# Softmax denominators: the last two key blocks summed on ScalarE out of the maximum pass

## Chip, core and metric

One core of a Trainium2 chip. The metric is the device time of one execution in microseconds (us), as the median of several executions; the profile is of one more execution of the same program.

## What is computed

The input is x, two images of 256 channels and 64x64 pixels. Layer 0 is attention over the 4096 pixels with 8 heads of 32 channels, followed by a masked mix with x; layer 1 is a chain of convolutions. What matters here:

```python
q = proj(Wq, bq) / math.sqrt(hd)          # (16, 4096, 32): 2 images x 8 heads
k = proj(Wk, bk)
v = proj(Wv, bv)
attn = jax.nn.softmax(jnp.einsum('bnd,bmd->bnm', q, k), axis=-1)
fuse = jnp.einsum('bnm,bmd->bnd', attn, v)
```

All of it is float32. The softmax of a query n needs the largest score over all 4096 keys m, and the sum of the exponentials over all keys.

## The kernel before

The program has a setup and projection phase, the attention phase (from about 230 to 3660 us) and an image phase with the convolutions. The change touches only the attention phase.

**Units.** Two heads are worked on together (a pair), for 512 queries at a time. That makes 8 pairs x 8 chunks = 64 units, and every unit has the same work:

- The maximum pass ("m" in the order): for each of 2 heads and 4 groups of 128 queries (8 sub-blocks, called hn) one matmul for each of 8 blocks of 512 keys, so 64 matmuls of 128 queries x 512 keys into PSUM (L654-659). They rotate through four banks, `mx`. VectorE reduces each to a column of maxima (L831), and when all 64 are there one small reduction makes the negated maxima (L836). SyncE then moves them with eight DMAs of 128 single numbers each into an extra row of the queries (`row`, L549-557), so that the score matmuls come out with the maximum subtracted.
- The scores ("s"): 64 matmuls of 128 keys x 512 queries (L645-651), which rotate through three banks, `st`. ScalarE turns each into probabilities in SBUF with an Exp (L786); the probabilities lie in a ring of 16 key tiles x 2 heads.
- The values ("V", L661-671): 16 steps, each the four matmuls of two key tiles and two heads, written as 32 columns each and accumulated in the one bank `acc`. Every such matmul stands in the trace as two instructions, so a V has eight.
- The sums ("S", L673-691): the denominators. GpSimd adds the probability tiles up in groups `GROUPS = [4,4,4,4,4,4,2,2]` (20 adds of 128x1024, L505), which covers 28 of the 32 key tiles; the four tiles left over are taken as they are. A matmul by ones then sums over the keys: 6 steps of the size of a V, into the same bank `acc`.

After the last V ScalarE copies the numerators out of `acc` (L761, two copies, after score `NUM_AFTER`), after the last S the denominators (L766, after score `DEN_AFTER`). The denominators go through DRAM (L563, L565), VectorE adds their parts and takes the reciprocal (L812, L815, placed in its own stream at block `INVERT`), and GpSimd scales the numerators (L859, L862, after add `SCALE_AFTER`).

**Order.** TensorE's program is written out by hand in the string `ORDER` (L388), one letter for each step, the same for every unit. It runs ahead: at its start `SCORES_AHEAD` scores of this unit and `BLOCKS_AHEAD` maximum blocks of the next unit have been done already, so its later letters belong to the next unit's scores and to the maximum blocks of the unit after that. Each engine works strictly through its own stream; semaphores are waited for in it.

```python
def max_block(v, p, gp, j):
    pe.wait_ge(mx_taken, MAXMM * v + j + 1)      # bank j % 4 has been reduced
...
act.wait_ge(scores, TILES * u + i + 1)           # score i is in its bank
if h == 0:
    buffer_free(u, s)                            # the ring slot has been used
```

SyncE's stream for a unit (L580-595) is: store and reload the previous unit's denominators (`normalize`), then the eight DMAs of `row`, the loads of later queries, the store of a finished unit.

## Time and profile before

| | us |
|---|---|
| median of 3 runs (4120.0 to 4120.87) | 4120.01 |
| the profiled execution | 4121.6 |
| its span, first to last instruction | 4119.8 |

| engine | busy, us | share of the span |
|---|---|---|
| TensorE matmul (PE) | 3956.2 | 96% |
| TensorE weight load (PEld) | 2046.8 | 50% |
| VectorE (DVE) | 2992.0 | 73% |
| ScalarE (ACT) | 2377.2 | 58% |
| GpSimd (POOL) | 3263.9 | 79% |

How to read it: L831 is line 831 of the kernel; busy times leave out waits; matmuls are pipelined, so that a matmul's row lasts longer than the distance to the next one, and the distance between two starts is what it costs. A row of the timeline may merge several instructions of one kind (x12), as one stretch from the start of the first. The clock is the one granted to TensorE: 1.00 is 2.4 GHz, 0.50 is 1.2 GHz.

### The profile page before, as it was taken

The page shows a single profiled execution, that of the slowest core. Times are in us where ns is not written, and L with a number is a line of the kernel's source. Part 1 is how long each engine was busy: PE and PEld are TensorE (multiplying, and loading weights), DVE is VectorE, ACT ScalarE, POOL GpSimd, SP SyncE. Part 2 cuts the span into 40 slices and gives each one's busy share as a digit, 9 for nine tenths or more (in the row PEclk, how much of TensorE's full clock was granted, in tenths as well). Part 3 has the DMA queues.
Part 4 walks back from the last instruction along what each step waited for, and adds up shares of the span by engine and source line. Part 5 has one row for each costly group of instructions (what it writes and reads, how often), then busy time and mean ns, then how long its engine had stood idle before and what let it go on. Part 6 is the DMA issues. An engine that isn't in the chain of part 4 may idle for free. (4 is left out here: it accounts for less than half of the span.)

```text
span 4119.8 us, 82469 instructions
## 1 busy us (share of the span) xinstructions
PE 3956.2 (96%) x20853; PEld 2046.8 (50%) x20853; DVE 2992.0 (73%) x5094; ACT 2377.2 (58%) x4488; POOL 3263.9 (79%) x1488
## 2 busy tenths in 40 slices
PE   7979999999999999999999999999999999959797
PEld 4535555555555555555555555555555555424343
DVE  3257777777777777777777777777777777518989
ACT  1216666666666666666666666666666666621213
POOL 3428999999999999999999999999999999940000
PEclk9959999999999999999999999999999999979898
DMA  6941110111011101110111011101110000022021
GB/s 199 283 116 40 39 24 22 30 39 31 22 33 42 31 19 32 42 32 22 31 42 32 22 33 42 31 22 32 42 32 22 22 22 21 10 58 76 26 77 41
DMA packets 223398, 188.86 MB, mean 46 GB/s; under 512 B 124434, under 2 KB 149188, under 8 KB 222916
## 3 DMA queue, kind: packets, MB, share of 16 engines
q1 hardware_dynamic: 223108, 185.67, 16.9%
q8 instruction: 100, 1.64, 0.2%
q14 instruction: 190, 1.56, 0.1%
HBM read 124.06 MB, written 61.21 MB: 45 GB/s over the span
## 5 line engine op out<-in xcount | busy, mean ns | idle before, releaser
L831 DVE TENSOR_REDUCE block_max<-mx 128x1 f32<-128x512 f32 x4096 | 2513.7, 681 | 798.6 <-PE mx L657 788.9
L786 ACT ACTIVATE prob<-st 128x512 f32<-128x512 f32 x4096 | 2140.4, 607 | 1152.9 <-PE st L650 1141.0
L505 POOL TENSOR_TENSOR prob_sum<-prob_sum,prob 128x1024 f32<-128x1024 f32 x768 | 1819.6, 2386 | 10.3 <-PE acc L689 10.2
L650 PE MATMUL st<-queries,keys 97*128 97x512 f32 x4096 | 1589.9, 410 | 5.4 <-issue 2.9
L657 PE MATMUL mx<-keys,max_queries 96*128 96x512 f32 x4096 | 1557.5, 412 | 27.3 <-DMA keys<-k_scratch 27.2
L505 POOL TENSOR_TENSOR prob_sum<-prob 128x1024 f32<-128x1024 f32 x512 | 1220.2, 2383 | 224.4 <-PE acc L689 162.9
L650 PEld LDWEIGHTS st<-queries,keys 97*128 97x128 f32 x4096 | 768.5, 189 | 611.4 <-ACT prob L786 352.7
L669 PE MATMUL acc<-prob,values 128*32 128x512 f32 x8192 | 1000.2, 600 | 0.0
L657 PEld LDWEIGHTS mx<-keys,max_queries 96*128 96x128 f32 x4096 | 781.8, 192 | 374.1 <-issue 134.0
L669 PEld LDWEIGHTS acc<-prob,values 128*32 128x32 f32 x8192 | 207.5, 109 | 449.5 <-issue 260.4
L689 PE MATMUL acc<-prob_sum,ones 128*32 128x512 f32 x2048 | 234.8, 599 | 5.3 <-ACT num_part L761 4.7
L366 POOL TENSOR_TENSOR low<-full,high 128x512 fp32r<-128x512 f32 x64 | 81.3, 1270 | 130.0 <-DVE high L347 130.0
L1260 DVE SCALAR_TENSOR_TENSOR conv<-o,dtaps,conv 128x512 f32<-128x512 f32 x256 | 170.4, 738 | 6.4 <-ACT conv L1145 6.4
L1035 PE MATMUL front<-xf,wfT 128*128 128x512 f32 x256 | 115.7, 607 | 40.5 <-DVE wfT L1308 36.6
L1127 ACT ACTIVATE edge<-conv,nshift,nscale 128x512 f32 (+1 forms) x32 | 24.3, 806 | 193.4 <-DVE conv L1226 193.4
L689 PEld LDWEIGHTS acc<-prob_sum,ones 128*32 128x32 f32 x2048 | 60.2, 110 | 145.8 <-issue 137.1
L335 ACT ACTIVATE full<-pq,bqs 128x512 f32<-128x512 f32 x64 | 44.0, 687 | 150.1 <-PE pq L310 150.1
L689 PE MATMUL acc<-prob,ones 128*32 128x512 f32 x1024 | 121.6, 592 | 0.0
L1073 PE MATMUL back<-conv,baT 128*128 128x512 f32 x128 | 68.1, 681 | 45.5 <-DVE conv L1260 45.5
L1226 DVE SCALAR_TENSOR_TENSOR conv<-y,etaps,conv 128x512 f32<-128x512 f32 x160 | 107.3, 745 | 0.0
L347 DVE CAST high<-full 128x512 fp32r<-128x512 f32 x64 | 27.3, 427 | 109.1 <-ACT full L335 109.1
L1035 PEld LDWEIGHTS front<-xf,wfT 128*128 128x128 f32 x256 | 49.7, 195 | 104.9 <-issue 102.8
(106 smaller groups left out, 1193.8 us busy)
## 6 DMA issues: line engine op xcount, KB each, us to landing
max_queries<-q_scratch SPq DMA_DIRECT2D x384, 64.0 KB, 1.9
queries<-q_scratch SPq DMA_DIRECT2D x384, 64.0 KB, 1.9
keys<-k_scratch SPq DMA_DIRECT2D x168, 128.0 KB, 2.5
x<-in_x SPq DMA_DIRECT2D x18, 512.0 KB, 4.3
q_scratch<-high SPq DMA_DIRECT2D x32, 256.0 KB, 4.3
k_scratch<-high SPq DMA_DIRECT2D x16, 512.0 KB, 4.9
q_scratch<-low SPq DMA_DIRECT2D x32, 256.0 KB, 5.1
k_scratch<-low SPq DMA_DIRECT2D x16, 512.0 KB, 4.9
```

What stands on the lines that cost most here:

```text
L366: nc.gpsimd.tensor_tensor(low[p][:, k, :], full[p][:, k, :], high[p][:, k, :].bitcast(F32), ALU.subtract).then_inc(low_ready, 1)
L505: nc.gpsimd.tensor_tensor(psum[k][:, :, :], a, prob[:, (first + i) % RING, :, :], ALU.add).then_inc(added[False], 1)
L650: nc.tensor.matmul(st[bank(i, p)][:, :], kk[gp][:, h, s * P:(s + 1) * P], qq[p][:, h, :], start=True, stop=True).then_inc(scores, 1)
L657: nc.tensor.matmul(mx[j % MAX_BANKS][:, :], qm[p][:, h, ns * P:(ns + 1) * P], kk[gp][0:SPLIT, h, blk * CH:(blk + 1) * CH], start=True, sto ...
L669: mm = nc.tensor.matmul(acc[HD * i:HD * (i + 1), :], vv[gp][:, h, 2 * q + a, :], prob[:, (2 * q + a) % RING, h, :], start=(q == 0), stop=( ...
L689: mm = nc.tensor.matmul(acc[HD * n:HD * (n + 1), :], ones[:, :], src[a][:, h, :], start=(i == 0), stop=(i == SUMS - 1))
L786: nc.scalar.activation(prob[:, s % RING, h, :], st[bank(i, p)][:, :], ACT.Exp).then_inc(exp_done, 1)
L831: nc.vector.tensor_reduce(bmax[p][:, j // MB, j % MB:j % MB + 1], mx[j % MAX_BANKS][:, :], AX.X, ALU.max).then_inc(mx_taken, 1)
L1035: mm = nc.tensor.matmul(front[p][ot][:, :], keep["wf"][:, kt, ot * P:(ot + 1) * P], xf[p][:, kt, :], start=(kt == 0), stop=(kt == 2 * CT - 1))
L1073: mm = nc.tensor.matmul(back[p][ot][:, :], keep["ba"][:, kt, ot * P:(ot + 1) * P], conv[p][:, kt, :], start=(kt == 0), stop=(kt == CT - 1))
L1226: nc.vector.scalar_tensor_tensor(out=as_rows(conv[p][:, ct, :]), in0=inner(y, ct, c, k=k), scalar=keep["etaps"][:, ct, k:k + 1], in1=as_ro ...
L1260: nc.vector.scalar_tensor_tensor(out=dst, in0=inner(o1, ct, c, k=i + 1), scalar=keep["dtaps"][:, ct, i + 1:i + 2], in1=dst, op0=ALU.mult, ...
```

## The change

ScalarE sums the last two key blocks (blocks 6 and 7 of each hn, 1024 keys) straight from the maximum pass. For this the four `mx` banks become one tensor. VectorE reduces blocks 0 to 5 one by one, and 6 and 7 in one instruction of 1024 columns, all of them negated; right after it, still within the same hn, it reduces the seven columns to that hn's negated maximum. ScalarE then takes one Exp over the two banks (1024 columns) with that maximum as bias, writes it back into the same two banks and gives the sum out as an accumulated column (`sum_tail`). TensorE may overwrite these two banks only when that Exp has finished. The eight columns of a unit go to DRAM with one DMA of 128x8 single numbers, and are added as a third part of the denominator. In return the key tiles 24 to 31 fall out of the sums: GpSimd has 6 groups and 18 adds, and TensorE 3 S steps. The values still use all 32 tiles. The negated maxima are buffered twice. The order is written anew.

```diff
-GROUPS = [4, 4, 4, 4, 4, 4, 2, 2]
+GROUPS = [4, 4, 4, 4, 4, 4]
-PLAIN = MT - sum(GROUPS)
+TAIL = 2
+SUMMED = MT - TAIL * NSUB
+PLAIN = SUMMED - sum(GROUPS)
+HN = 2 * NSUB
+TAKES = MB - TAIL + 1
-ORDER = ("ssmmmsmsVsmsmsmmsmsmsVsmssmmsmsmmssmVsmsmsmsmsmsmsmsVVsmsmsmsmsmsmsmsmsVVms"
-         "mssmmmsmsmVsmsmsmsmmsmssVVVmssmsmmsmsmsmsVVVVmsmsmsmsmsmmssmsmVmmsmssSSSSSS")
-SCORES_AHEAD = 18
+ORDER = ("msmVVVmssmsmmsmsmsmsmsVVsmsmsmsmsmsmsmsmsVVsmsmsmsmsmsmsmsmsVVmsmsmsmsmsm"
+         "smsmsVVVsmmssmmsmsmsVsssmmVmsmsmsmsmmssmVVsmsmsmssmmmssmmSSSmsmsmssmmsmsms")
+SCORES_AHEAD = 23
-INVERT = 61
-NUM_AFTER, DEN_AFTER = 14, 18
-SCALE_AFTER = 17
+INVERT = 57
+NUM_AFTER, DEN_AFTER = 12, 15
+SCALE_AFTER = 12
+TAIL_AHEAD = 0
+TAIL_AFTER = [0, 8, 15, 23, 30, 39, 48, 57]
+TAIL_FIRST = BLOCKS_AHEAD // MB
...
-        dcol = sb("den_col", [P, 2, 2 * CH // P])
+        dcol = sb("den_col", [P, 3, 2 * CH // P])
-        mx = [ctx.enter_context(nc.psum_tensor(f"mx{i}", [P, CH], F32)) for i in range(MAX_BANKS)]
+        mx = ctx.enter_context(nc.psum_tensor("mx", [P, MAX_BANKS, CH], F32))
...
             def row(u, p):
-                sp.wait_ge(nmax_ready, u + 1)
+                sp.wait_ge(nmax_ready, HN * (u + 1))
...
+                tail = scratch["den"][bass.ds(u, 1), 4 * CH:6 * CH]
+                sp.wait_ge(tail_summed, HN * (u + 1))
+                sp.dma_start(tail.rearrange("a (i n) -> n (a i)", n=P), part[p][:, :],
+                             allow_slow_non_contiguous=True).then_inc(part_stored, 16)
...
             def normalize(v):
...
                 sp.wait_ge(den_stored, 16 * (v + 2))
-                sp.dma_start(dcol[:, :, :], row.rearrange("a (e p k) -> (a p) e k", e=2, p=P)).then_inc(dcol_loaded, 16)
+                sp.wait_ge(part_stored, 16 * (v + 2))
+                sp.dma_start(dcol[:, :, :], row.rearrange("a (e p k) -> (a p) e k", e=3, p=P)).then_inc(dcol_loaded, 16)
...
-            def max_block(v, p, gp, j):
-                pe.wait_ge(mx_taken, MAXMM * v + j + 1)
+            def max_block(v, p, gp, j, first=False):
+                last, older = (j - MAX_BANKS) // MB, (j - MAX_BANKS) % MB
+                if older < MB - TAIL:
+                    pe.wait_ge(mx_taken, TAKES * HN * v + (TAKES * (last + 1) + older + 1))
+                elif j >= MB or not first:
+                    pe.wait_ge(tail_summed, HN * v + (last + 1))
...
-                            pe.wait_ge(row_loaded, ROW_INC * (u + 3))
+                            pe.wait_ge(row_loaded, ROW_INC * (u + 2))
...
+            def sum_tail(v, p, hn, first=False):
+                if hn == 0 and not first:
+                    act.wait_ge(part_stored, 16 * v)
+                if hn or not first:
+                    act.wait_ge(tail_summed, HN * v + hn)
+                act.wait_ge(nmax_ready, HN * v + hn + 1)
+                nc.scalar.activation(mx[:, MAX_BANKS - TAIL:MAX_BANKS, :], mx[:, MAX_BANKS - TAIL:MAX_BANKS, :], ACT.Exp,
+                                     bias=nmax[p][:, hn:hn + 1].bitcast(F32),
+                                     accum_out=part[p][:, hn:hn + 1]).then_inc(tail_summed, 1)
...
+                    for x, at in enumerate(TAIL_AFTER):
+                        d, hn = divmod(TAIL_AHEAD + x, HN)
+                        if i == at and d < ahead and (prev or TAIL_AHEAD + x >= TAIL_FIRST):
+                            sum_tail(u + 1 + d, (p + 1 + d) % 2, hn)
...
+            for n in range(HN + TAIL_FIRST):
+                sum_tail(n // HN, n // HN, n % HN, first=n < HN)
             unit(0, 0, prev=False)
...
                 for j in range(MAXMM):
-                    dve.wait_ge(mx_ready, MAXMM * v + j + 1)
-                    nc.vector.tensor_reduce(bmax[p][:, j // MB, j % MB:j % MB + 1], mx[j % MAX_BANKS][:, :], AX.X,
-                                            ALU.max).then_inc(mx_taken, 1)
+                    hn, blk = j // MB, j % MB
+                    if blk < MB - TAIL or blk == MB - 1:
+                        k = min(blk, MB - TAIL)
+                        banks = mx[:, blk % MAX_BANKS - blk + k:blk % MAX_BANKS + 1, :]
+                        dve.wait_ge(mx_ready, MAXMM * v + j + 1)
+                        nc.vector.tensor_reduce(bmax[p][:, hn, k:k + 1], banks.rearrange("p b n -> p (b n)"), AX.X,
+                                                ALU.max, negate=True).then_inc(mx_taken, 1)
+                    if blk == MB - 1:
+                        dve.wait_ge(mx_taken, TAKES * (HN * v + hn + 2))
+                        nc.vector.tensor_reduce(nmax[p][:, hn:hn + 1], bmax[p][:, hn, :], AX.X,
+                                                ALU.min).then_inc(nmax_ready, 1)
                     between(v, j, prev, older)
-                dve.wait_ge(mx_taken, MAXMM * v + MAXMM + MAX_BANKS)
-                dve.wait_ge(row_loaded, ROW_INC * (v + 1))
-                nc.vector.tensor_reduce(nmax[:, :], bmax[p][:, :, :], AX.X, ALU.max, negate=True).then_inc(nmax_ready, 1)
```

## Rows read from the trace of the kernel before

**Rows 1.** Windows: busy of PE, PEld, DVE, ACT, POOL; then PEclk, DMA share, GB/s.

```profile
400.00:3400.00 3000.00, 2997.09 (x17445) 1581.05 (x17438) 2273.38 (x3835) 2004.34 (x3837) 2835.09 (x1263) 1.00 0.13 31
240.00:300.00 60.00, 59.05 (x101) 29.06 (x102) 57.70 (x97) 1.64 (x4) 1.61 (x1) 0.50 0.28 65
```

**Rows 2.** Groups by line, 1000 to 1448 us: count, busy, mean ns, idle before.

```profile
L831 DVE TENSOR_REDUCE block_max<-mx 128x1 f32<-128x512 f32 x549 | 337.2, 681 | 104.3 <-PE mx L657 102.9
L786 ACT ACTIVATE prob<-st 128x512 f32<-128x512 f32 x549 | 287.1, 607 | 145.2 <-PE st L650 143.7
L505 POOL TENSOR_TENSOR prob_sum<-prob_sum,prob 128x1024 f32<-128x1024 f32 x104 | 246.4, 2387 | 1.3 <-PE acc L689 1.3
```

**Rows 3.** Timeline of TensorE: start, length, instruction (stretches of one unit).

```profile
1507.14 0.64 PE L650 MATMUL st<-queries,keys 97*128 97x512 f32 x2
...
1512.99 0.73 PE L650 MATMUL st<-queries,keys 97*128 97x512 f32 x2
...
1518.74 0.39 PE L650 MATMUL st<-queries,keys 97*128 97x512 f32 x1
...
1520.40 0.40 PE L657 MATMUL mx<-keys,max_queries 96*128 96x512 f32 x1
...
1530.47 0.40 PE L657 MATMUL mx<-keys,max_queries 96*128 96x512 f32 x1
...
1533.98 0.42 PE L650 MATMUL st<-queries,keys 97*128 97x512 f32 x1
...
1536.18 0.50 PE L657 MATMUL mx<-keys,max_queries 96*128 96x512 f32 x1
1536.52 0.40 PE L650 MATMUL st<-queries,keys 97*128 97x512 f32 x1
```

**Rows 4.** Timeline of VectorE around the end of a unit's maximum pass.

```profile
332.14 0.22 DVE L836 TENSOR_REDUCE negated_max<-block_max 128x8 fp32r<-128x64 f32 x1
...
1484.47 7.91 DVE L831 TENSOR_REDUCE block_max<-mx 128x1 f32<-128x512 f32 x13 [0.30 <-PE mx L657]
...
1534.81 1.26 DVE L831 TENSOR_REDUCE block_max<-mx 128x1 f32<-128x512 f32 x2
1536.21 0.22 DVE L836 TENSOR_REDUCE negated_max<-block_max 128x8 fp32r<-128x64 f32 x1
1536.72 7.93 DVE L831 TENSOR_REDUCE block_max<-mx 128x1 f32<-128x512 f32 x13 [0.28 <-PE mx L657]
```

**Rows 5.** Groups by line and shape, outside the attention: biased and accumulating instructions.

```profile
L335 ACT ACTIVATE full<-pq,bqs 128x512 f32<-128x512 f32 x64 | 44.0, 687 | 150.1 <-PE pq L310 150.1
...
L1127 ACT ACTIVATE edge<-conv,nshift,nscale 128x512 f32<-128x512 f32 x16 | 12.2, 806 | 44.8 <-DVE conv L1226 44.8
...
L1209 DVE DVE_READ_ACCUMULATOR y<-diff,xf x16 | 1.3, 81 | 0.0
```

**Rows 6.** Single lines: duration ns min/median/max of the smallest instructions.

```profile
L795 ACT ACTIVATE exp_warm<-ones x1: 203/203/203, 229.0 to 229.0; 128x1 f32<-128x1 f32 x1
...
L812 DVE TENSOR_REDUCE den_sum<-den_col x64: 156/157/172, 383.1 to 3656.5; 128x8 f32<-128x16 f32 x64
```

**Rows 7.** Timeline of SyncE's DMA issues: the maximum rows of two units.

```profile
332.38 4.98 SPq L555 DMA_DIRECT2D queries<-negated_max  x8
...
1536.54 1.66 SPq L572 DMA_DIRECT2D fuse<-rec_scratch  x2
1538.24 5.04 SPq L555 DMA_DIRECT2D queries<-negated_max  x8
```

**Rows 8.** The row's DMAs (L555), 1000 to 1448 us, 72 of them.

```profile
DMA to landing us min/median/max: 1.9/2.0/3.1
```

**Rows 9.** Timeline of attention's beginning and end, several engines.

```profile
241.70 38.35 DVE L831 TENSOR_REDUCE block_max<-mx 128x1 f32<-128x512 f32 x64 [13.86 <-PE mx L657]
...
3649.25 1.28 POOL L859 TENSOR_TENSOR num<-num_part 64x512 f32<-64x512 f32 x1
...
3652.32 0.59 ACT L766 COPY den<-acc 128x512 f32<-128x512 f32 x1 [7.86 <-PE acc L689]
```

More of the change, by code:

```diff
@@ L441, in attention_phase @@
         ones = sb("ones", [P, HD])
-        bmax = [sb(f"block_max{p}", [P, 2 * NSUB, MB]) for p in range(2)]
-        nmax = sb("negated_max", [P, 2 * NSUB], F32R)
+        bmax = [sb(f"block_max{p}", [P, HN, TAKES]) for p in range(2)]
+        nmax = [sb(f"negated_max{p}", [P, HN], F32R) for p in range(2)]
+        part = [sb(f"tail_sum{p}", [P, HN]) for p in range(2)]
         warm = sb("exp_warm", [P, 1])
@@ L469, in attention_phase @@
         nmax_ready = sem("negated_max_ready")
+        tail_summed = sem("tail_summed")
+        part_stored = sem("tail_sum_stored")
         row_loaded = sem("max_row_loaded")
@@ L523, in _ @@
             sp.sem_inc(fuse_stored, 16)
[L524 removed]
+            sp.sem_inc(part_stored, 16)
             def load_kv(g, p, part, parts=KV_PARTS, first=None):
@@ L562, in normalize @@
                 sp.wait_ge(den_ready, v + 2)
-                sp.dma_start(row.rearrange("a (i n) -> (a i) n", i=4), den[0:P:HD, :]).then_inc(den_stored, 16)
+                sp.dma_start(row[:, 0:4 * CH].rearrange("a (i n) -> (a i) n", i=4), den[0:P:HD, :]).then_inc(den_stored, 16)
                 sp.wait_ge(den_stored, 16 * (v + 2))
-                sp.dma_start(dcol[:, :, :], row.rearrange("a (e p k) -> (a p) e k", e=2, p=P)).then_inc(dcol_loaded, 16)
+                sp.wait_ge(part_stored, 16 * (v + 2))
+                sp.dma_start(dcol[:, :, :], row.rearrange("a (e p k) -> (a p) e k", e=3, p=P)).then_inc(dcol_loaded, 16)
                 sp.wait_ge(rcol_ready, v + 1)
@@ L737, in _ @@
                     pe.wait_ge(kv_loaded[0], KV_INC)
-                max_block(0, 0, 0, j)
+                max_block(0, 0, 0, j, first=True)
             pe.wait_ge(qm_loaded[1], Q_INC)
@@ L744, in _ @@
             pe.wait_ge(q_loaded[0], Q_INC)
-            pe.wait_ge(row_loaded, ROW_INC * 2)
+            pe.wait_ge(row_loaded, ROW_INC)
             for i in range(SCORES_AHEAD):
@@ L776, in buffer_free, with unit @@
                     act.wait_ge(added[own], ADDS[own] * v + adds_until(k, i))
-                else:
+                elif t < SUMMED:
                     act.wait_ge(sums_done, SUMS * v + (len(GROUPS) + t - GROUP_END[-1]) // 2 + 1)
-            def unit(u, p, prev=True):
+            def sum_tail(v, p, hn, first=False):
[7 more added lines that the diff above has]
+                                     accum_out=part[p][:, hn:hn + 1]).then_inc(tail_summed, 1)
+            def unit(u, p, prev=True, ahead=2):
                 for i in range(TILES):
@@ L795, in _ @@
             nc.scalar.activation(warm[:, :], ones[:, 0:1], ACT.Exp)
+            for n in range(HN + TAIL_FIRST):
+                sum_tail(n // HN, n // HN, n % HN, first=n < HN)
             unit(0, 0, prev=False)
-            with act.Fori(0, UNITS // 2 - 1) as u2:
+            with act.Fori(0, UNITS // 2 - 2) as u2:
                 unit(u2 * 2 + 1, 1)
                 unit(u2 * 2 + 2, 0)
-            unit(UNITS - 1, 1)
+            unit(UNITS - 3, 1)
+            unit(UNITS - 2, 0, ahead=1)
+            unit(UNITS - 1, 1, ahead=0)
             copy_num(UNITS - 1)
@@ L805, in _ @@
         def _(dve):
-            dve.sem_inc(mx_taken, MAX_BANKS)
+            dve.sem_inc(mx_taken, TAKES)
             if PIECES:
@@ L822, in between @@
                         invert(v - 2)
-                for at, piece in zip(ADD_AFTER, PIECES):
+                for at, piece in zip([], PIECES):
                     if prev and j == at:
```

10 lines of the change are left out of this document (5 added, 5 removed).

## The prediction

> **What bounds the kernel now.** I read the windows first: from 400 to 3400 us TensorE has no idle time (2997 of 3000 us) at a granted clock of 1.00 [rows 1]. No other engine is near: GpSimd is busy for 95% of that stretch, VectorE for 76%, ScalarE for 67%. The groups by line say what the others do with their time: ScalarE and VectorE wait mostly for matmuls, GpSimd's chain stops only for the sums [rows 2].
>
> A busy share does not say what a step costs, so I took the distances between matmul starts [rows 3]. A maximum block or a score costs 0.234 us (15 distances in the 3.51 us from 1530.47 to 1533.98). One V between two of them: 1520.40 - 1518.74 less two distances, 1.19 us. Two V: 1536.52 - 1533.98 less two, 2.07. Six S: 1513.33 - 1507.37 (the second score of the row at 1507.14 starts 0.23 into it, the one after the sums 0.34 after 1512.99) less two, 5.49. So a group of k steps costs 0.33 + 0.86 k. A unit before has 128 blocks and scores, 22 V and S, in 10 groups: 29.95 + 18.92 + 3.30 = 52.17 us. The unit's real length, between the reductions at 1484.47 and 1536.72, is 52.25 us [rows 4]. TensorE's own stream explains it to 0.1 us: nothing is waited for, and what leaves the stream is gained until another engine comes up.
>
> **Part 1: three S less.** Three of six S go, and by the new order the V and S stand in 9 groups, not 10: 3 x 0.86 + 0.33 = 2.91 us less for a unit. TensorE's content becomes 49.36 us with the same remainder of 0.1. No letter "m", "s" or "V" is saved.
>
> **Part 2: GpSimd.** Two adds of 2.386 us go [rows 2]: 18 x 2.386 plus scaling of 2 x 1.28 [rows 9] is 45.5 us. It may start on a unit's sums only when the first S of the unit before has freed a buffer (1 us after its start), and must be through before the third S, 1.7 us after the next first S: its cycle is at least 44.8 us, under 49.4. Its last add uses tile 23, whose ring slot ScalarE writes again at score 14 of the next unit, 0.6 us after the first S: GpSimd is through 46.4 us after the S before, which leaves some 3 us. It stays hidden, with 4 us of room.
>
> **Part 3: VectorE.** For each hn, six reductions spaced 0.60 us (13 in 7.91 us, [rows 4]), one of 1024 columns, one small one. From 16 columns in 0.157 [rows 6] to 512 in 0.681 us [rows 2] a column costs 1.06 ns, so 1024 take 1.22. With the small one at 0.16 and the 0.14 us gap that a reduction after its predecessor's end shows [rows 4] this is 5.1 us, 41 for a unit: hidden in 49.4.
>
> **Part 4: the Exp over 1024 columns.** No such instruction is in the trace. From 1 column in 0.203 [rows 6] to 512 in 0.607 us [rows 2] a column costs 0.79 ns; with a bias column 512 take 0.687 [rows 5]. So 1024 take 1.09 us, and the reading of an accumulator, which VectorE's rows have at 0.08 [rows 5], makes 1.17. The low end is 1.09; the high end is twice the costliest 512 columns (0.806, [rows 5]) and 0.08, 1.7 us. I take 1.2, near the row with a bias. ScalarE then has 64 x 0.52 (287.1 us for 549, [rows 2]) + 1.8 for copies + 9.6 = 45 us: hidden, but at 91%.
>
> **Part 5: the handover, the real question.** The banks of blocks 6 and 7 now come free for blocks 2 and 3 of the next hn only after: block 7's matmul, 1024-column reduction, small reduction, Exp. Counted from the start of block 7: the four single reductions from block 2 on (start 0.54 after it, 1536.18 to 1536.72, [rows 3, 4]) put the long reduction at +0.49; its end +1.71; gap and small reduction +2.01; Exp from +2.06 to +3.26; TensorE again at +3.31 (each handover at 0.05: the matmul that starts at 1536.18 and takes 0.50 is followed by its reduction at 1536.72, 0.04 later, [rows 3, 4]). Against that stands what the order puts between block 7 and the next block 2. For hn 4 to 5: block 7, s m s m s, VV, s: 7 x 0.234 + 2.07 = 3.7. All eight: 3.7, 3.7, 3.45, 4.55, 4.0, 3.7, 3.85, 4.1 (hn 4 to 5 first). All are above 3.31, the closest by 0.14. So I cost the wait at nothing; its cover is the V or SSS in each gap. If the Exp takes 1.7 the chain is 3.8 us and four gaps run short, by 0.35 and three times 0.1: some 0.7 us a unit. The longer, later Exps also push the numerator copies: S needs them, and following ScalarE from score 9 on I find the copies 0.15 us late.
>
> The profile and the Trainium skill can be set against each other here. The rows show four banks freed 0.6 us apart and no TensorE wait left from that. The skill's page "Perfetto Trace Analysis" (Optimizing Tensor Performance, Matmuls) wants groups to rotate through PSUM banks so that evacuating one overlaps the next group's matmuls, and "PSUM — Partial Sum Buffer" (Summary) asks to evacuate promptly; both speak against holding two banks for a chain. By them the handovers would bubble in every hn, which is the slower rival below; by the rows the gaps cover it.
>
> **Part 6: the maximum row.** The next unit's scores wait for eight DMAs. SyncE issues them only when all eight maxima are there, 0.02 us after the last reduction (332.36 to 332.38, [rows 4, 7]); the last of eight starts 7/8 of 5.04 us later [rows 7] and lands after 2.0 [rows 8]. From block 7 of hn 7: 2.01 + 0.02 + 4.41 + 2.0 = 8.44. The order has 18 distances, VVV and V between it and score 0: 4.21 + 2.91 + 1.19 = 8.31; the old one has 12.5 by the same count. So TensorE waits about 0.2 us here, and somewhat more where SyncE comes late from the previous unit's loads, which already take from 1536.54 to 1538.20: 0.3 on the mean. Low end 0; high end 1.5, if the DMAs land as late as the slow ones (3.1 us, [rows 8]).
>
> The ninth DMA, 1024 single numbers, is not in the trace. The nearest row, 128 such numbers, takes 0.63 us to issue; between that and eight times it, 5 us. Behind it in SyncE's queue are the loads for later units and the store, then the denominators some 8 us later, which themselves are used 25 us after: hidden at both ends.
>
> **The sum.** A unit: 49.36 + 0.15 + 0.3, and 0.1 for handovers that I did not follow: 49.9 against 52.27, 2.37 less, times 62 units that run in full: -147. At the beginning 96 maximum blocks ran alone at VectorE's 0.60 us (38.35 for 64, [rows 9]) at half clock [rows 1]. Now each hn is a closed chain of 5.9 us (0.54 to the first reduction and, at half clock, an estimated 0.2 more, four spacings, 1.22 + 0.30, Exp, handovers) against 4.8: 11 x 1.1 = +12. Five more scores run ahead at ScalarE's 0.52 us [rows 2]: +2.6. The last unit ends with GpSimd's chain and 3.1 us of S behind it (3649.25 to 3652.32, [rows 9]); two adds and two S go: -6.7. Together -139: the profiled execution, 4121.6, becomes 3982; the medians lie 1.6 lower, 3980.
>
> **Rivals.**
> - *Clean* (0.20): DMAs land in time, ScalarE keeps up; 49.4 a unit, 31 us better: about 3948. For it: ends of parts 4 and 6. Against: 8.44 over 8.31.
> - *Mine* (0.42): 49.6 to 50.3, 3962 to 4005.
> - *The Exp is long or the row late* (0.26): the Exp at 1.5 to 1.7 or a row wait over 1 us: 50.4 to 51.5, 4010 to 4080. For it: the accumulator's cost on ScalarE is unseen, ScalarE at 91% has little to catch up with.
> - *Slower* (0.08): the bank handover. The shortfalls over the eight gaps reach 2.9 us when the chain is 4.2 us, which is an Exp of 2.1 us or the same loss before it. At 4.5 us they are 5.0, and the unit 54.9: 4290. Against: even the high end is 1.7.
> - *No gain* (0.04): the shortfalls just eat the saving, or another engine sets 52 us (4112 to 4128). That the change doesn't do what it says I don't see: the S are out of the order by count.
>
> **Numbers.** What a measurement can tell from no change is 0.2%, 8 us. Likeliest 3980. The range runs from 3942, the clean case less a little, to 4055, inside the long-Exp case, and leaves out about 2 in 10. Faster 0.88, same 0.04, slower 0.08.
>
> **What would show it.** In the changed profile: the unit length between two like reductions, 49.9; groups of S with 24 instructions; the Exp on `mx` at 1.2 us; TensorE's wait on it near none, on the DMA of the row 0.2 to 0.3 a unit; the small reduction's end within 2.1 us of block 7's start. I am wrong if the Exp is over 1.5 us, if TensorE waits for `mx` banks in most hn, or if GpSimd's sums are what S waits for.

## The result, and the profile after

The changed kernel takes 4378.78 us in the median of four runs (4375.59 to 4384.86), the kernel before 4120.32 beside it: the ratio is 1.0629 [1.061, 1.0647]. I had forecast 3980 and a gain; it lost 6.3%. The profiled execution took 4384.86 us, with a span of 4383.0.

The page of the changed kernel (busy us and share of the span) first:

```profile
PE 3919.6 (89%) x19317; PEld 2054.6 (47%) x19317; DVE 3055.2 (70%) x5030; ACT 2936.8 (67%) x5512; POOL 2961.7 (68%) x1360
...
DMA packets 298174, 189.55 MB, mean 43 GB/s; under 512 B 199186, under 2 KB 223940, under 8 KB 297668
...
L805 ACT ACTIVATE mx<-mx,negated_max 128x1024 f32<-128x1024 f32 x512 | 561.7, 1097 | 105.1 <-DVE negated_max L878 84.8
...
L805 ACT ACTIVATION_READ_ACCUMULATOR mx<-mx,negated_max 128x1 f32 x512 | 104.9, 205 | 0.0
```

No engine is busier than TensorE was before, and TensorE's share has fallen from 96% to 89%: it waits now. The windows (columns as in [rows 1]) say when. The first row is the stretch of [rows 1]; then come two consecutive units and, within the second, six microseconds before, in and after a hole:

```profile
400.00:3400.00 3000.00, 2751.57 (x14837) 1470.66 (x14836) 2156.22 (x3498) 2317.39 (x4399) 2371.30 (x1061) 0.94 0.19 29
1503.70:1553.80 50.10, 49.71 (x282) 26.96 (x281) 40.53 (x67) 43.54 (x83) 44.76 (x21) 1.00 0.19 22
1553.80:1615.10 61.30, 53.31 (x282) 28.24 (x281) 40.77 (x67) 43.88 (x84) 44.77 (x21) 0.92 0.16 19
1588.00:1594.00 6.00, 4.45 (x26) 1.90 (x18) 3.52 (x6) 2.50 (x5) 6.00 (x3) 1.00 0.51 42
1594.00:1600.00 6.00, 0.00 (x0) 0.00 (x0) 0.71 (x2) 0.40 (x1) 2.54 (x2) 0.76 0.74 68
1600.00:1606.00 6.00, 5.75 (x20) 3.08 (x24) 2.71 (x4) 4.55 (x9) 0.00 (x0) 0.50 0.13 48
```

A unit, read as the distance between two stores of denominators, lasts 50.1 us here and the next one 61.2. That goes on through the phase: of the first 60 distances the 1st, 3rd, 5th ... have a median of 50.9 us and the others of 60.9. The short one comes near the unit that I forecast (49.9). The long one has a hole in which TensorE does nothing for six microseconds and after which its granted clock is 0.50 (1.2 GHz) until about 1606 us. The timelines of that hole, SyncE's issues, ScalarE's instructions and TensorE's:

```profile
1585.79 1.89 SPq L564 DMA_DIRECT2D queries<-negated_max  x3
1587.88 0.44 SPq L569 DMA_DIRECT2D den_scratch<-tail_sum  x1
1588.52 2.85 SPq L554 DMA_DIRECT2D max_queries<-q_scratch  x6
...
1592.12 0.60 ACT L815 ACTIVATE prob<-st 128x512 f32<-128x512 f32 x1
1599.60 2.08 ACT L815 ACTIVATE prob<-st 128x512 f32<-128x512 f32 x4 [6.88 <-issue]
...
1593.33 0.40 PE L675 MATMUL mx<-keys,max_queries 96*128 96x512 f32 x1
1600.25 0.80 PE L664 MATMUL st<-queries,keys 97*128 97x512 f32 x1 [6.52 <-ACT prob L815]
```

TensorE waits for ScalarE's Exp, and ScalarE for nothing that the profile shows ("issue"). The place is the same in every second unit: the first Exps of ScalarE's loop body, which covers two units, so it is reached once in two units, just after the jump back. (One more unit is long, 61.6 us at 2565 us: there TensorE waited 9.4 us for the DMAs of the maximum row.) The stand shown ends 11.7 us after the new DMA of 1024 single numbers (L569) was issued, and in the hole the DMA engines are busy for 0.74 of their time, against 0.08 to 0.15 in the microseconds in which the row's DMAs are issued alone. The packet records of the trace say with what: of the 71 us of packet time that begin between 1594 and 1600 us, 68 belong to packets of 2048 bytes, the size that the loads issued behind the new DMA are made of. They take up to 2.06 us each there, where the median is 0.084. The single numbers' own packets take 0.007 to 0.009 us in the median. So it is what comes behind them that becomes slow. Two things coincide: the new DMA, and a jump that needs its instructions.

One TensorE group that I had feared stays small. The waits of TensorE from 400 to 3400 us (in total, times, longest):

```profile
PE st L664 <- ACT prob L815: 171.1, 38, 8.1
PE st L664 <- DMA queries<-negated_max: 32.0, 53, 9.4
PE mx L675 <- ACT mx L805: 29.7, 21, 4.2
```

The first row is the hole, the second the maximum row (Part 6), the third the handover of the two banks (Part 5). The holes are 171 us; the stretch at half clock behind each makes the long units 10 us longer than the short ones, and not 6.5.

### The profile page after: what moved, and what is told of

It is laid out like the page before. It is cut to its first block and busy times, and to the rows that moved or that the text cites. A ratio compares the mean times of both kernels' runs of the same rounds, so it can differ in the third digit from the quotient of the medians.

```text
span 4383.0 us, 80623 instructions
## 1 busy us (share of the span) xinstructions
PE 3919.6 (89%) x19317; PEld 2054.6 (47%) x19317; DVE 3055.2 (70%) x5030; ACT 2936.8 (67%) x5512; POOL 2961.7 (68%) x1360
## 5 line engine op out<-in xcount | busy, mean ns | idle before, releaser
L874 DVE TENSOR_REDUCE block_max<-mx 128x1 f32<-128x512 f32 (+1 forms) x3584 | 2527.2, 761 | 1002.6 <-PE mx L675 984.4
L664 PE MATMUL st<-queries,keys 97*128 97x512 f32 x4096 | 1635.9, 421 | 238.2 <-ACT prob L815 201.9
L675 PE MATMUL mx<-keys,max_queries 96*128 96x512 f32 x4096 | 1610.8, 420 | 87.3 <-ACT mx L805 52.7
L514 POOL TENSOR_TENSOR prob_sum<-prob 128x1024 f32<-128x1024 f32 x384 | 914.6, 2382 | 771.0 <-PE acc L707 696.5
L664 PEld LDWEIGHTS st<-queries,keys 97*128 97x128 f32 x4096 | 788.9, 194 | 822.2 <-ACT prob L815 376.1
L675 PEld LDWEIGHTS mx<-keys,max_queries 96*128 96x128 f32 x4096 | 810.3, 198 | 464.9 <-ACT mx L805 207.5
L687 PE MATMUL acc<-prob,values 128*32 128x512 f32 x8192 | 1026.0, 620 | 0.0
L805 ACT ACTIVATE mx<-mx,negated_max 128x1024 f32<-128x1024 f32 x512 | 561.7, 1097 | 105.1 <-DVE negated_max L878 84.8
L707 PE MATMUL acc<-prob_sum,ones 128*32 128x512 f32 x1536 | 190.6, 631 | 12.4 <-ACT num_part L779 8.1
L805 ACT ACTIVATION_READ_ACCUMULATOR mx<-mx,negated_max 128x1 f32 x512 | 104.9, 205 | 0.0
```

The costliest lines, as they stand in the source:

```text
L514: nc.gpsimd.tensor_tensor(psum[k][:, :, :], a, prob[:, (first + i) % RING, :, :], ALU.add).then_inc(added[False], 1)
L664: nc.tensor.matmul(st[bank(i, p)][:, :], kk[gp][:, h, s * P:(s + 1) * P], qq[p][:, h, :], start=True, stop=True).then_inc(scores, 1)
L675: nc.tensor.matmul(mx[:, j % MAX_BANKS, :], qm[p][:, h, ns * P:(ns + 1) * P], kk[gp][0:SPLIT, h, blk * CH:(blk + 1) * CH], start=True, sto ...
L687: mm = nc.tensor.matmul(acc[HD * i:HD * (i + 1), :], vv[gp][:, h, 2 * q + a, :], prob[:, (2 * q + a) % RING, h, :], start=(q == 0), stop=( ...
L707: mm = nc.tensor.matmul(acc[HD * n:HD * (n + 1), :], ones[:, :], src[a][:, h, :], start=(i == 0), stop=(i == SUMS - 1))
L805: nc.scalar.activation(mx[:, MAX_BANKS - TAIL:MAX_BANKS, :], mx[:, MAX_BANKS - TAIL:MAX_BANKS, :], ACT.Exp, bias=nmax[p][:, hn:hn + 1].bit ...
```

## The experiments

### Without the DMA, the DMA alone, and the same bytes in longer runs

First run: the DMA goes. The last two key blocks are then missing from the denominators; nothing else is left out.

```diff
-                sp.dma_start(tail.rearrange("a (i n) -> n (a i)", n=P), part[p][:, :], ...)
+                sp.sem_inc(part_stored, 16)
```

> The changed kernel without the DMA that carries the 128x8 tail sums to DRAM; the denominators then lack the tail's part (keys 3072 to 4095). Theory A (that DMA's 1024 single-number writes keep the DMA engines busy for some 10 us, and ScalarE's next instructions, fetched through the same engines when its loop over two units jumps back, wait behind them): every unit takes 50 us, no idle time of ScalarE over 1 us with nothing to wait for, TensorE's clock at 1.00, total 3985 to 4010. Theory B (ScalarE's loop body has grown, and its jump back costs 7 us whatever the DMAs do): every second unit stays at 61 us, total 4350 to 4380. Theory C (the handover of the banks, with an Exp of 1.3 us, is the loss): total over 4300, waits on the Exp over mx in every unit.

4038.72 us, 0.9805 [0.9786, 0.9825]. The long units are gone, but for the two in which TensorE's own loop jumps back (58.5 and 57.0 us). All of the change but this DMA, and the third of the reload that brought its numbers back, gains 2%. My range (3985 to 4010) was missed by 29 us; what they are comes under "What is left to the forecast".

Second run: the kernel before, with that DMA alone (from a constant tile to a DRAM tensor that nobody reads), behind the row.

```diff
+                sp.dma_start(scratch["extra"][bass.ds(u, 1), :].rearrange("a (i n) -> n (a i)", n=P), ones[:, 0:8],
+                             allow_slow_non_contiguous=True).then_inc(extra_stored, 16)
```

> The kernel before with one DMA more in each unit, after the eight of the maximum row: 128x8 single numbers from a constant tile to a DRAM scratch that nobody reads. Theory A: ScalarE's jump back lies within 4 us of that DMA here too (first score of a unit at about +3 us), so every second unit loses 7 to 11 us: 4340 to 4460. Theory B or C: the DMA is hidden, 4120 to 4125.

4301.33 us, 1.0443 [1.0422, 1.0464]. The kernel before has units of 52.3 us with not one exception over 54; now 21 of the first 60 are over 57. From its timelines and, below, its windows (a long unit):

```profile
1443.45 0.44 SPq L560 DMA_DIRECT2D extra_scratch<-ones  x1
...
1453.27 2.08 ACT L791 ACTIVATE prob<-st 128x512 f32<-128x512 f32 x4 [8.10 <-issue]
...
1453.92 0.80 PE L655 MATMUL st<-queries,keys 97*128 97x512 f32 x1 [5.17 <-ACT prob L791]
```

```profile
1448.00:1453.00 5.00, 0.74 (x4) 0.27 (x2) 1.96 (x4) 0.00 (x0) 5.00 (x3) 0.98 0.25 32
1453.00:1459.00 6.00, 5.08 (x19) 2.65 (x23) 2.08 (x3) 3.87 (x7) 5.86 (x4) 0.50 0.43 104
```

There is no tail Exp, no shared bank and no new order here, and the picture is that of the changed kernel: a stand at ScalarE's jump back, a wait of TensorE, the clock at 0.50 behind it. Of the stand of 8.1 us, 5.2 reach TensorE. This DMA alone costs 181 us, less than I had expected (4340 to 4460): nine of the 30 units that begin behind the jump are not long here. The handover is not the cause.

Third run: the changed kernel, with the eight numbers of a query row written side by side. They reach other queries than their own; no work is left out.

```diff
-                sp.dma_start(tail.rearrange("a (i n) -> n (a i)", n=P), part[p][:, :],
-                             allow_slow_non_contiguous=True).then_inc(part_stored, 16)
+                sp.dma_start(tail.rearrange("a (n i) -> n (a i)", n=P), part[p][:, :]).then_inc(part_stored, 16)
```

> The changed kernel with the same 4 KB to the same place in DRAM, but as 128 runs of 8 numbers instead of 1024 single numbers; the sums then reach other queries than their own. Theory A, if the number of writes is what costs: the DMA takes a tenth of the time, units 50 to 51 us, total 3990 to 4030. If it is the write to DRAM as such, or the bytes: 4380 as the changed kernel. Theory B or C: 4380.

4039.67 us, 0.9808 [0.9788, 0.9827]: the same 4 KB in 128 runs of 32 bytes cost nothing that the comparison with the first run shows (like there, the time is above my range, 3990 to 4030). It is not the bytes, nor that a DMA stands there.

### The jump back and the place

Now the other half of the coincidence. ScalarE's loop gets a body of four units in the changed kernel, so that it jumps back half as often:

```diff
-            with act.Fori(0, UNITS // 2 - 2) as u2:
-                unit(u2 * 2 + 1, 1)
-                unit(u2 * 2 + 2, 0)
+            with act.Fori(0, UNITS // 4 - 1) as u4:
+                for d in range(4):
+                    unit(u4 * 4 + (d + 1), (d + 1) % 2)
```

> The changed kernel with ScalarE's loop holding four units and jumping back 15 times instead of 30; the slow DMA stays. If the 7 us stand behind ScalarE's jump back (theory A): only one unit in four is 60 us long, total 4378 less about 15 times 10: 4200 to 4240. If any fetch of instructions, wherever it falls, runs into the DMA: as many slow units or more, 4350 to 4450.

4223.42 us, 1.0255 [1.0235, 1.0276]; every fourth unit is long (mostly 59.6 to 61.5 us) and not every second. Half of the jumps, and about half of the loss against the first run: 185 of 340 us are left. The first run still jumps twice as often; by the 22 us that a body of four units saves without the slow DMA (4030.0 to 4007.84, below) I estimate that 207 of the 340 us are left against a kernel with the same body.

Then the changed kernel's DMA is taken out of `row` and put behind the loads of the next queries:

```diff
+            def tails(u, p):
                 tail = scratch["den"][bass.ds(u, 1), 4 * CH:6 * CH]
                 sp.wait_ge(tail_summed, HN * (u + 1))
                 sp.dma_start(tail.rearrange("a (i n) -> n (a i)", n=P), part[p][:, :], ...)
...
+                tails(u + 1, 1 - p)
                 if keys:
```

> The changed kernel with the same DMA of 1024 single numbers to DRAM, issued after the six loads of the next queries, some 8 us later and so about 3 us after ScalarE's jump back. If the coincidence of the two is what costs: ScalarE's idle time there is gone, units of 50 to 52 us, 4040 to 4100, unless TensorE's or GpSimd's jump back, which come next, now meet it. If the DMA costs wherever it is: 4380.

4077.59 us, 0.9901 [0.9881, 0.9921]. The same DMA, 300 us cheaper, some 40 above the kernel without it. What the DMA costs depends on what stands beside it in time. From 400 to 3400 us no 2048-byte packet takes over 1 us here, while in the changed kernel 1473 of 27348 do.

### What makes the DMA so long

Half of the numbers (128x4), in the kernel before:

```diff
-                sp.dma_start(scratch["extra"][bass.ds(u, 1), :].rearrange("a (i n) -> n (a i)", n=P), ones[:, 0:8],
+                sp.dma_start(scratch["extra"][bass.ds(u, 1), 0:CH].rearrange("a (i n) -> n (a i)", n=P), ones[:, 0:4],
```

> The kernel before with one more DMA of 128x4 single numbers (512 of them, half of the other run's 1024), after the row. With 1024 numbers ScalarE stands up to 9.7 us after its jump back and the time is 181 us over the kernel before. If the jump back waits for the single numbers to be written, the stand is about half, 4 to 6 us, of which the part that ScalarE's cushion does not take (3 to 4 us of the 9.7 did not reach TensorE there) is small: 4125 to 4200 us. If it is the DMA as such and not the count of its numbers, 4280 to 4310.

4293.68 us, 1.0429 [1.0412, 1.0446]: as slow as with 1024. My explanation by the count of numbers fell here. What the two have in common is where the numbers go: 128 partitions write into the same 512 bytes (a row of 128 numbers), four or eight such stretches side by side. Three more runs of the kernel before take that apart:

```diff
-    scratch["extra"][bass.ds(u, 1), :].rearrange("a (i n) -> n (a i)", n=P), ones[:, 0:8],
+    scratch["extra"][bass.ds(u, 1), :].rearrange("a (n i q) -> n (a i) q", n=P, q=P)[:, :, 0:1], ones[:, 0:8]...,
```

```diff
-    scratch["extra"][bass.ds(u, 1), :].rearrange("a (i n) -> n (a i)", n=P), ones[:, 0:8],
+    scratch["extra"][bass.ds(u, 1), 0:P].rearrange("a (i n) -> n (a i)", n=P), ones[:, 0:1],
```

The third is the first with `q=2` for `q=P`, so that the numbers stand 8 bytes apart.

> The kernel before with one more DMA of 1024 single numbers a unit, as in the first run of this kind (4301 us), but each number goes to a place of its own, 512 bytes from the next; there, and in the run with 512 numbers (4294), 128 numbers of 128 partitions go side by side into the same 512 bytes. If the time comes from many writes into the same stretch of DRAM, it goes away here: 4118 to 4150. If it comes from single numbers as such, whatever their count and place, it stays: 4280 to 4310.

> The kernel before with one more DMA of 128x1 single numbers to DRAM, all side by side in one stretch of 512 bytes. If the hold is set by the 128 writes into one stretch (1024 and 512 numbers are 8 and 4 such stretches, with about the same stand), it stays nearly whole: 4230 to 4300. If it grows with the count, but flattens above 512, it is small: 4118 to 4160. The maximum row is eight such DMAs, but into SBUF, and costs no such thing.

> The kernel before with one more DMA of 1024 single numbers to DRAM, 8 bytes apart, the 8 of a partition next to one another: 64 numbers in 512 bytes, of 8 partitions. 1024 separate writes as before, but fewer partitions meet in one stretch. If the count of separate writes decides, 4280 to 4310. If the meeting of 128 partitions in one stretch decides, it is less than half of it: 4118 to 4200.

The last two columns are counted in the packet records of the traces, from 400 to 3400 us: packets of an instruction queue (q14, 8192 bytes, 155 to 164 of them) that took over 2 us, and 2048-byte packets (28170 to 29672 of them, for the most part of loads) that took over 1 us. In the kernel before there are none of either.

| DMA beside the kernel before | numbers | of them in one 512 bytes | us | ratio | slow instruction packets | slow 2048-byte packets |
|---|---|---|---|---|---|---|
| 128x8, rows of 128 | 1024 | 128 | 4301.33 | 1.0443 [1.0422, 1.0464] | 21 | 646 |
| 128x4, rows of 128 | 512 | 128 | 4293.68 | 1.0429 [1.0412, 1.0446] | 29 | 351 |
| 128x1 | 128 | 128 | 4202.74 | 1.0208 [1.0191, 1.0225] | 39 | 1344 |
| 128x8, 8 bytes apart | 1024 | 64 | 4172.93 | 1.0132 [1.0115, 1.0149] | 23 | 181 |
| 128x8, 512 bytes apart | 1024 | 1 | 4116.28 | 0.9997 [0.9987, 1.0006] | 0 | 1 |

1024 separate single numbers cost nothing when each has its 512 bytes, and 128 of them cost 85 us in one stretch. ScalarE's waits from 400 to 3400 us show the stand with 128 numbers and none with 1024 spread ones, and the page gives the spread ones 3.1 us to landing (those 8 bytes apart take 6.4, by the same count of numbers). First the kernel with 128 numbers, then the one with 1024 that have 512 bytes each, and its row of the page's DMA issues:

```profile
ACT prob L791 <- POOL prob_sum L506: 81.6, 16, 5.6
ACT prob L791 <- issue: 22.0, 4, 6.5
```

```profile
ACT prob L791 <- PE st L655: 967.7, 516, 5.7
```

```profile
extra_scratch<-ones SPq DMA_DIRECT2D x64, 4.0 KB, 3.1
```

(Where ScalarE's stand is put down to GpSimd's `prob_sum`, as in the first of these rows, it is the same place and the same stand: the profile names the semaphore that came last.) So the price goes by how many separate writes meet in one stretch of DRAM. The number of partitions alone does not set it: with the numbers 8 bytes apart 64 writes of only 8 partitions meet in 512 bytes and cost 55 us, while the runs of 32 bytes in the changed kernel, 16 writes of 16 partitions in 512 bytes, cost nothing (the writes are longer there too, which was not taken apart). From one such stretch to four the price doubles (85 to 173 us over the kernel beside each), while from four to eight it stays (8 us more). How long a stretch has to be for writes to meet was not varied: 512 bytes are what a row of 128 numbers fills, and a shorter one would fit the runs as well. My expectation of the 8-byte run held, and the spread one, 2 us under its range (4118 to 4150), is no different from the kernel beside it (4117.69). The time with 128 numbers fell between my two (4230 to 4300 and 4118 to 4160), 27 us under the first.

The Trainium skill's page "DMA: Bandwidth & Descriptors" (Specifications) says that transfers under 512 bytes are done as a read-modify-write. That fits a penalty for meeting in 512 bytes, but by it alone the 1024 spread numbers would pay as well, and they pay nothing; it is the meeting that the runs show.

That ScalarE waits for its instructions is what the traces' packets say too. The list of DMA queues on each page has two instruction queues among the 16 DMA engines' work. One of them moves the same packets with and without the 1024 single numbers, but takes a larger share of the engines' time with them (packets, MB, share; the kernel before, then the same with the DMA). From 400 to 3400 us its packets take 158 us together instead of 70:

```profile
q14 instruction: 190, 1.56, 0.1%
```

```profile
q14 instruction: 190, 1.56, 0.3%
```

The usual packet of this queue takes 0.3 to 0.7 us, and none in the kernel before took longer. In the kernel with the 1024 numbers (4301.33) 18 stands of over 6.5 us lie between 400 and 3400 us, and in 14 of them such a packet begins within 0.35 us of the stand's beginning and takes 3.2 to 4.0 us. What fills the rest of a stand no record shows. The changed kernel has 11 of 179 packets over 2 us there (the longest 7.57), without the DMA or with its rows of 32 bytes none. Their count alone does not give the time (39 go with 85 us in the table, 21 with 181): it matters where they fall. That the slow packets are ScalarE's is inferred, from the place of the stand, from this agreement in time and from the loss that goes with the number of jumps; why writes that meet hold up the packets behind them was not tried.

### Getting the change without the DMA through DRAM

The first way sends the eight columns inside SBUF, with eight DMAs of 128 numbers to a tile of 128x8, and adds it to the denominators with one VectorE addition:

```diff
+                for i in range(HN):
+                    sp.dma_start(tcol[p][P // HN * i:P // HN * (i + 1), :]..., part[p][:, i:i + 1]..., ...)
...
+                nc.vector.tensor_tensor(dall[:, :], dsum[:, :], tcol[p][:, :], ALU.add).then_inc(dall_ready, 1)
```

> The whole computation, with the tail sums moved from SBUF to SBUF (eight DMAs of 128 single numbers, as those of the maximum row) and added by VectorE with one small addition more. Theory A, if single numbers written into SBUF go as quickly as those of the maximum row (share of the DMA engines about 0.1): units 50 us, total 3990 to 4015, under the kernel before by 2.5 to 3%. If single numbers cost the same wherever they land: 4300 or more. Theory B or C: 4380.

4404.32 us, 1.0688 [1.0653, 1.0722]: slower still, with units of 55 to 61 us throughout (median 56.6). By my expectation this would mean that single numbers cost the same wherever they land; the timelines show another cause. Those of VectorE, GpSimd and TensorE in one unit:

```profile
1537.77 0.16 DVE L853 TENSOR_REDUCE den_sum<-den_col 128x8 f32<-128x16 f32 x1
1538.03 5.64 DVE L857 TENSOR_TENSOR den_all<-den_sum,tail_col 128x8 f32<-128x8 f32 x1
...
1540.05 2.38 POOL L518 TENSOR_TENSOR prob_sum<-prob_sum,prob 128x1024 f32<-128x1024 f32 x1
1542.35 1.30 POOL L910 TENSOR_TENSOR num<-num_part 64x512 f32<-64x512 f32 x1
...
1544.55 0.80 PE L679 MATMUL mx<-keys,max_queries 96*128 96x512 f32 x1 [4.34 <-DVE block_max L881]
```

An addition of eight numbers in a partition takes 5.64 us (4.92 in the median of the 64, and 0.17 at the least), and ends at 1543.67, when GpSimd's row of operations does (1542.35 + 1.30). VectorE reduces nothing meanwhile and TensorE runs out of banks. The Trainium skill's page "SBUF — State Buffer" (SBUF: two separate sides) says that a VectorE instruction with two SBUF inputs takes the pair of ports that GpSimd uses, as a lock. The row agrees, and the wait is longer than one of GpSimd's adds (2.38 us); the kernel before and the changed one have no VectorE instruction with two SBUF inputs in this phase, and their small ones take 0.16 to 0.20 us.

So the eight DMAs write into a third part of `den_col` (now two buffers), and the one reduction adds all three:

```diff
-        dcol = sb("den_col", [P, 3, 2 * CH // P])
+        dcol = [sb(f"den_col{p}", [P, 3, 2 * CH // P]) for p in range(2)]
...
+                    sp.dma_start(dcol[p][P // HN * i:P // HN * (i + 1), 2, :]..., part[p][:, i:i + 1]..., ...)
```

> The whole computation. As in the run before, the tail sums go from SBUF to SBUF in eight DMAs, but straight into the third part of a doubled den_col, so that VectorE sums all three parts in its one small reduction, and the addition of two SBUF tiles (den_all, 5.6 us in that run while GpSimd adds) is gone. Theory A with that addition as the only cause of the 56 us units: units of 50 and 51 us as without the DMA, total 4035 to 4050. If the eight DMAs themselves cost: 56 us units again, 4400.

4041.83 us, 0.9815 [0.9798, 0.9831], with the whole computation, as expected (4035 to 4050); so the eight DMAs inside SBUF cost some 3 us against the first run. The row that took 5.64 us is a reduction of 0.17:

```profile
1569.59 0.17 DVE L851 TENSOR_REDUCE den_sum<-den_col 128x8 f32<-128x24 f32 x1
```

### What is left to the forecast

This kernel is 62 us above the forecast of 3980. Its units have medians of 50.5 and 51.0 us. Two causes were tried on it. First the maximum row: the first six of its DMAs are issued as their maxima come, before SyncE waits for the reciprocals. The row gets a semaphore for each of the two query buffers.

```diff
-            def row(u, p):
-                sp.wait_ge(nmax_ready, HN * (u + 1))
+            def row(u, p, lo=0, hi=HN):
...
+                        if not lo <= i < hi:
+                            continue
+                        sp.wait_ge(nmax_ready, HN * u + i + 1)
...
+                if u is not None:
+                    row(u, p, 0, EARLY)
...
-                row(u + 1, 1 - p)
+                row(u + 1, 1 - p, 0 if first else EARLY)
```

> The run with the sums inside SBUF (e5) and the maximum row's DMAs issued as each sub-block's maximum is ready, the first six before SyncE waits for the reciprocal; semaphores by parity. My account of the unit says that TensorE waits 0.3 to 0.6 us a unit for that row and ScalarE's first score stands behind it: units 0.4 to 0.7 us shorter than in e5, total 4000 to 4020. If the row is hidden anyway: the same as e5. If the order of SyncE's stream delays the reciprocal or the loads: longer.

4030.0 us, 0.9782 [0.9766, 0.9798]: 12 us better, less than expected (4000 to 4020). The short units fell to 49.8 and the wait for the row is gone from TensorE, but every second unit stayed at 51.3. In ScalarE's timeline these differ from the short ones in one row, again at the jump back (the second; the first is its twin in a short unit):

```profile
1526.38 0.60 ACT L824 ACTIVATE prob<-st 128x512 f32<-128x512 f32 x1 [0.88 <-PE st L672]
...
1577.48 0.60 ACT L824 ACTIVATE prob<-st 128x512 f32<-128x512 f32 x1 [2.26 <-POOL prob_sum L516]
```

To tell the jump from GpSimd's adds, to which the wait is put down, the loop body was made four and then twenty units long (the version with the rows as they come, 15 and 3 passes):

```diff
-            with act.Fori(0, UNITS // 2 - 2) as u2:
+            with act.Fori(0, (UNITS - 4) // 20) as un:
+                for d in range(20):
+                    unit(un * 20 + (d + 1), (d + 1) % 2)
```

> The version with the rows as they come (4030.0 us) has units of 49.8 us and, in turn, of 51.1 to 51.5; in the longer ones ScalarE stands 2.3 us after the first Exp of its loop body, where it stands 0.9 in the others. If that is ScalarE's jump back, a body of four units has it half as often: 15 of 30 units lose 1.4 us less, 4030 - 21 = about 4009 (4002 to 4016), and every fourth unit is the longer one. If it is GpSimd's adds (which the wait is put down to), nothing changes: 4026 to 4034, and every second unit stays longer.

> The same with a body of twenty units, three passes. If only the jump back costs, 27 of 30 longer units are gone: 4030 - 27 x 1.4 = about 3992 (3985 to 4002), and units of 49.8 but for two. If ScalarE's straight code has a price of its own (more code to be fetched than before between two jumps, the same amount for a unit), the time stays above 4005. If GpSimd's adds are the cause, 4026 to 4034.

4007.84 us (0.9736 [0.972, 0.9753]) and 3993.39 us (0.97 [0.9684, 0.9716]). Both as the jump has it, and not as GpSimd's adds would (4026 to 4034): with four units every fourth is a long one, with twenty of the distances at ScalarE's jump only the 20th and the 40th are left (51.4 and 51.2; the 16th and the 32nd, 57.1 and 56.3, are at TensorE's own jump). The last is the fastest kernel of this study, 3.0% under the kernel before, with the whole computation. Its windows and TensorE's waits (one of its units; then 400 to 3400 us):

```profile
1480.00:1530.00 50.00, 49.82 (x283) 27.09 (x282) 40.73 (x68) 43.83 (x85) 45.05 (x22) 1.00 0.11 23
...
400.00:3400.00 3000.00, 2977.91 (x16761) 1612.97 (x16750) 2423.74 (x3947) 2610.59 (x4966) 2680.28 (x1197) 1.00 0.14 32
```

```profile
PE mx L683 <- issue: 8.2, 2, 4.2
PE mx L683 <- ACT mx L814: 2.7, 2, 1.4
```

Last, what the sum output of the Exp costs. In the version with the rows as they come and the body of two units, the tail's Exp gives out no sum, and its part of the denominator is a constant; so the last two key blocks are missing from the denominators here.

```diff
-                                     bias=nmax[p][:, hn:hn + 1].bitcast(F32),
-                                     accum_out=part[p][:, hn:hn + 1]).then_inc(tail_summed, 1)
+                                     bias=nmax[p][:, hn:hn + 1].bitcast(F32)).then_inc(tail_summed, 1)
```

> The version with the rows as they come, but the Exp over the two banks gives out no sum (the tail's part of the denominator is a constant 1.0 for each query and part, so the last two key blocks are missing from the sums). It measures what the read of the accumulator costs: the Exp's row without its 0.20 us read. If the handover of the two banks still costs TensorE something, the unit of 49.8 falls towards the content of 49.36, by 0.2 to 0.4 us: 4005 to 4018. If the handover is hidden, as Part 5 had it, the time stays: 4026 to 4034.

4014.75 us, 0.975 [0.9734, 0.9766], 15 us under its neighbour with the sum (4030.0): inside the band that I gave for a handover that still costs. But its units say less than the band: the short ones went from 49.8 to 49.7 us, the long from 51.3 to 51.1. The eight reads of 0.205 us are 1.6 us of ScalarE a unit, of which about 0.2 reach the end. The handover is hidden nearly whole.

## Why the prediction was wrong

**The step that failed is Part 6, its ninth DMA.** I wrote that its cost lay "between that and eight times it, 5 us" and was "hidden at both ends". That counted how long SyncE needs to issue it, from the issue row of 128 numbers, and asked only who is queued behind it on SyncE. The issue took 0.44 us, less than the 0.63 of the nearest row, and it did not matter. What it did to the DMA engines was not in my sum, and neither was ScalarE's jump back as somebody who waits for them. The row that I took as nearest, 128 single numbers of `row`, goes into SBUF; the 128-number DMA to DRAM (85 us for the kernel) shows that it was no neighbour. What the runs showed in its place: writes that meet in one stretch of DRAM slow the packets behind them, and ScalarE stands some 7 us at its jump back. The DMA cost 340 us: 4378.78 against 4038.72 without it. All but 3 us of the gap to the version with the sums in `den_col` (4041.83) lies between the first and the last denominators (3540.6 us against 3199.6 in the profiles).

**The slower rival had the right sign and the wrong place.** At 8 in 100 it made 4290 us of a handover of two banks. Its own test, TensorE's wait on `mx`, is 29.7 us of the 3000, and the DMA alone in the old kernel makes the same holes.

**The rest, part by part, held but for the Exp's price:**

- Part 1: for a forecast 49.9 us the short units have a median of 50.1 in the kernel without the DMA (50.9 in the changed kernel, the shortest 50.1). In the last versions, where the row comes early and TensorE waits for almost nothing, they take 49.8, for a content of 49.36.
- Part 2: GpSimd is busy for 44.8 us a unit (45.5 worked out) and waits for TensorE's S, not the other way; hidden.
- Part 3: the 1024-column reduction takes 1.22 us and the small one 0.16, as worked out (timeline of VectorE, in the first version through SBUF, whose maximum pass is that of the changed kernel):

```profile
1535.22 1.22 DVE L881 TENSOR_REDUCE block_max<-mx 128x1 f32<-128x1024 f32 x1
```

- Part 4: the Exp takes 1.10 us (forecast 1.09 for the columns), but ScalarE's read of the accumulator takes 0.205, where I had put VectorE's 0.08. So 1.30 and not 1.2, 0.8 us more a unit; of the whole read, 1.6 us a unit, about 0.2 costs time.
- Part 5: hidden, at 2.7 us in 3000 in the best version. With the body of two units the waits on the Exp over `mx` are 22.7 us (sums in `den_col`) and 39.6 us (rows as they come); they all but go with the jumps.
- Part 6, the row: 25.9 us in 57 waits in the version with the sums in `den_col`, 0.4 a unit, where I had 0.3. In the changed kernel it is 32.0 us, of which one wait is 9.4.
- The beginning: the first denominators are stored 8.3 us later than before in the version with the sums in `den_col` (371.5 against 363.2), and 11.6 in the changed kernel. I had 14.6.

**What was missing beside the big step** is ScalarE's jump back by itself. It costs 1.3 to 1.5 us in every second unit, with no slow DMA near: in the kernel before ScalarE had 33% to spare and hid it, and with ScalarE at 88% of a unit (43.83 of 50 us) it does not. With most of that taken out, and the row's DMAs issued early, which the forecast did not have, 3993.39 stands against 3980. That its units are right to 0.1 us is in part luck: the sum had 0.3 for a row wait that is gone there, and too little for the Exp. The remaining 13 us are mostly two units of 56 to 57 us at TensorE's own jump back (two stands of up to 4.2 us; the kernel before had 53.8 there).

The clock made the loss larger. Each hole of 6 to 7 us was followed by a granted clock of 0.50, so the long units are 10 us longer (60.9 against 50.9) and not 6.5. I had reckoned with stalls that add up at face value.

## What to carry to other kernels

The time that a DMA takes on its issuing queue says nothing of what it does to the DMA engines. When a change adds one, ask who else needs them at that moment, an engine's jump back included, and whether many small writes fall close together in DRAM: a column of 128 numbers transposed into a row was the dearest form here (128 writes in 512 bytes), while through SBUF or in rows of 32 bytes the sums cost some 3 us or less. An engine that the change fills up loses the cushion that hid its loop's jump; a longer body is then worth trying.

## What the runs showed that I had not expected

- 128 single numbers written from 128 partitions into one stretch of 512 bytes of DRAM cost the kernel before 85 us over 64 times, 1024 of them in rows of 128 cost 181, and 1024 that stand 512 bytes apart cost none (4116.28 against 4117.69).
- The price shows in other DMAs' packets: 2048-byte ones, with a median of 0.084 us, took up to 5.1 us in the changed kernel, and 8192 bytes of instructions up to 7.6 us where 0.3 to 0.7 is usual.
- Beside the kernel before, the stands of over 6.5 us at the jump end 7.7 to 12.2 us after the DMA of 512 numbers is issued (median 9.2, 22 stands), and 9.2 to 11.4 us after that of 1024 (median 10.5, 21 stands).
- A VectorE addition of 128x8 with both inputs in SBUF takes 4.92 us in the median beside GpSimd's adds, and units of 56.6 us follow from it; a reduction in its place takes 0.17 us.
- A loop's jump back makes ScalarE stand about 1.4 us longer than straight code, with no slow DMA near.
